# Saving the halves of a key or query tile ahead of the load of the next weight tile, on the SyncE queue of a cross-attention kernel

## The reference

```python
Q = split_heads(query @ Wq.T + bq); K = split_heads(key @ Wk.T + bk); V = split_heads(value @ Wv.T + bv)
scores = einsum('bhqd,bhkd->bhqk', Q, K) / sqrt(32)
scores = where(mask[:, None, :, :] == 0, -1e9, scores)
attn = softmax(scores, axis=-1)
ctx = einsum('bhqk,bhkd->bhqd', attn, V).reshape(B, LQ, H)
x = ctx @ Wo.T + bo + query
out = (x - mean(x)) / sqrt(var(x) + 1e-5) * ln_g + ln_b
```

## Time and profile before

| | |
|---|---|
| median of 3 runs | 1682.52 us (1680.51 to 1682.59) |
| the profiled execution | 1682.58 us, of it the span of the core 1680.8 us |
| TensorE busy (matmul) | 1608.1 us, 96% |
| GpSimd, ScalarE, VectorE busy | 1408.6 us (84%), 1349.6 us (80%), 1168.9 us (70%) |
| granted TensorE clock, mean | 0.983 |
| DMA queue of SyncE, share of 16 engines | 66.5%, 325.94 MB |
| chain that ended last | TensorE 78%, DMA 12% (of it `stack_scratch<-qk_lo` 11%), VectorE 6% |

### The profile page before, as it was taken

One profiled execution on the slowest core, in us unless ns is written; L12 is line 12 of the kernel. 1 busy time (PEld: TensorE's weight loads), 2 busy tenths in 40 slices (PEclk: granted clock), 3 DMA queues, 4 the chain that ended last, 5 costly groups with the idle time before them and its releaser, 6 DMA issues.

```text
span 1680.8 us, 25568 instructions
## 1 busy us (share of the span) xinstructions
PE 1608.1 (96%) x7997; PEld 1029.3 (61%) x7997; DVE 1168.9 (70%) x2852; ACT 1349.6 (80%) x1555; POOL 1408.6 (84%) x875
## 2 busy tenths in 40 slices
PE   7879999999999999999999999999999999999986
PEld 5546666666666666666666666666666666665633
DVE  6647767767777676777767677676777767676744
ACT  3668888887889788788888878888888888878772
POOL 5558888898889989889898988989898997988683
PEclk9999999999999999999999999999999999999977
DMA  7886676776767677586777757667676867757401
GB/s 250 249 252 193 166 225 183 208 220 175 242 164 235 182 214 221 159 241 175 220 197 202 217 166 233 192 209 218 170 231 169 241 179 202 225 171 220 102 9 69
DMA packets 197479, 327.58 MB, mean 195 GB/s; under 512 B 39264, under 2 KB 39264, under 8 KB 197344
## 3 DMA queue, kind: packets, MB, share of 16 engines
q1 hardware_dynamic: 197344, 325.94, 66.5%
HBM read 236.72 MB, written 89.13 MB: 194 GB/s over the span
## 4 chain that ended last, share of the span: by engine, by line
PE 78%; DMA 12%; DVE 6%; POOL 2%; issue 1%; ACT 1%; SPq 0%; DVEq 0%; ACTq 0%; POOLq 0%
PE proj_bank L1099 37%; PE ring L973 12%; PE exp_banks L988 12%; PE ctx_bank L1004 12%; DMA stack_scratch<-qk_lo 11%; DVE qk_lo L817 2%; PE ring L1024 2%; DVE ring L776 2%; PE ring L1033 1%; DVE qk_hi L814 1%; DMA b_all<-ln_b_dram 1%; ACT qk_hi L663 1%; POOL total L497 1%; PE ctx_bank L1099 0%; POOL c_lo L475 0%
## 5 line engine op out<-in xcount | busy, mean ns | idle before, releaser
L776 DVE CUSTOM_DVE_ANT_0 ring<-ring,bias 128x512 f32<-128x512 f32 x1024 | 690.5, 711 | 308.0 <-PE ring L973 306.7
L643 ACT ACTIVATE probs<-exp_banks 128x1024 f32<-128x1024 f32 x512 | 524.5, 1025 | 226.2 <-PE exp_banks L988 223.9
L614 ACT CAST exp_banks<-biasT 128x1024 f32<-128x1024 bf16 x512 | 520.7, 1017 | 23.1
L973 PE MATMUL ring<-k_stack,q_stack 96*128 96x512 f32 x1024 | 333.3, 403 | 15.4 <-DVE maxes L776 10.9
L988 PE MATMUL exp_banks<-q_stack,k_stack 98*128 98x512 f32 x1024 | 327.6, 402 | 3.0 <-ACT exp_banks L614 3.0
L505 POOL TENSOR_TENSOR total<-total,probs 128x1024 f32<-128x1024 f32 x126 | 299.4, 2400 | 10.0 <-ACT probs L643 1.2
L497 POOL TENSOR_TENSOR total<-total,probs 128x2048 f32<-128x2048 f32 x63 | 290.4, 4609 | 11.5 <-ACT probs L643 2.9
L497 POOL TENSOR_TENSOR total<-probs 128x2048 f32<-128x2048 f32 x63 | 289.5, 4596 | 0.0
L1004 PE MATMUL ctx_bank<-probs,v 128*32 128x512 f32 x2048 | 278.5, 616 | 0.7 <-DVE recipT L843 0.7
L973 PEld LDWEIGHTS ring<-k_stack,q_stack 96*128 96x128 f32 x1024 | 194.8, 191 | 75.5 <-DVE maxes L776 25.0
L988 PEld LDWEIGHTS exp_banks<-q_stack,k_stack 98*128 98x128 f32 x1024 | 194.0, 191 | 58.5 <-issue 9.2
(11 more groups left out here) (131 smaller groups left out, 2248.8 us busy)
## 6 DMA issues: line engine op xcount, KB each, us to landing
w_tile<-w_scratch SPq DMA_DIRECT2D x240, 256.0 KB, 3.2
k_stack<-stack_scratch SPq DMA_DIRECT2D x192, 256.0 KB, 4.6
q_stack<-stack_scratch SPq DMA_DIRECT2D x192, 256.0 KB, 6.6
stack_scratch<-qk_hi SPq DMA_DIRECT2D x128, 256.0 KB, 2.9
stack_scratch<-qk_lo SPq DMA_DIRECT2D x128, 256.0 KB, 3.7
c_raw<-cT_dram SPq DMA_DIRECT2D x64, 256.0 KB, 3.7
x_raw<-xT_dram SPq DMA_DIRECT2D x64, 256.0 KB, 4.7
mask_raw<-mask_dram SPq DMA_DIRECT2D x64, 256.0 KB, 4.6
```

What stands on the lines that cost most here:

```text
L614: nc.scalar.copy(exp_banks[:, 2 - 2 * wave:4 - 2 * wave, :], biasT[:, kc:kc + 1, :].to_broadcast([P, 2, L])).then_inc(seeded, 1)
L643: nc.scalar.activation(probs[:, u % PS, 2 - 2 * wave:4 - 2 * wave, :], exp_banks[:, 2 - 2 * wave:4 - 2 * wave, :], ACT.Exp).then_inc(exps, 1)
L776: nc.vector.tensor_tensor_reduce(out=ring[:, n % 2], in0=ring[:, n % 2], in1=bias[:, c], scale=1.0, scalar=LOWEST, op0=ALU.subtract, op1=A ...
L973: nc.tensor.matmul(ring[:, n % 2], q_stack[0:3 * D, at, c * P:(c + 1) * P], k_stack[0:3 * D, at, :], start=True, stop=True).then_inc(ring_ ...
```

## The change

In each step, the halves of tile `y - 1` are now saved ahead of the load of the weights of tile `y + 1`. `load_weights` takes the part as an argument and is called twice in a row; its waits are thereby written twice, the second time already met.

```diff
-            def load_weights(tile):
+            def load_weights(tile, part):
                 i = PLAN.qk[tile]
                 if i < MADE:
                     return
                 sp.wait_ge(proj_done, PLAN.no[PLAN.qk_list[i - WS]] + 1)
                 sp.wait_ge(wk_scratch if tile[0] == "K" else wq_scratch, 2 * FULL)
                 w = (0 if tile[0] == "K" else NG) + tile[2]
-                for part in range(2):
-                    sp.dma_start(w_tile[:, i % WS, part].bitcast(FP32), w_scratch[w, :, part]).then_inc(
-                        w_loaded[i % WS][part], FULL)
+                sp.dma_start(w_tile[:, i % WS, part].bitcast(FP32), w_scratch[w, :, part]).then_inc(
+                    w_loaded[i % WS][part], FULL)
...
                 if PLAN.max_group(y) is not None:
                     store_maxes(PLAN.max_group(y))
-                tile = PLAN.tile(y + 1)
-                if tile and tile[0] in "QK":
-                    load_weights(tile)
                 tile = PLAN.tile(y - 1)
                 if tile and tile[0] in "QK":
                     keep_halves(tile)
                     if PLAN.qk[tile] < 2:
                         stack(tile[0], 0)
+                tile = PLAN.tile(y + 1)
+                if tile and tile[0] in "QK":
+                    load_weights(tile, 0)
+                    load_weights(tile, 1)
```

## The result

The changed kernel takes 1693.1 us, the median of 5 runs (1689.14 to 1698.57), against 1682.52 us before (5 runs, 1679.06 to 1685.25). The ratio is 1.0053, 95% interval 1.0034 to 1.0072: slower by 0.5% (the quotient of the two medians, 1.0063, lies inside the interval). The forecast was 1681.1 us, range 1670 to 1689. The profiled execution took 1693.56 us, its span 1691.8 us.

What follows compares the result with a forecast made beforehand. The prediction took TensorE's work and its waits for `qk_lo` (22.0 us in 27 events) to bound the kernel. Its sum was 1682.58 - 12.7 - 0.8 + 12.0 = 1681.1 us, range 1670 to 1689.

Steps and rivals of the forecast that it cites:

- Positions 6, 8, 9 and 10, other work behind the halves: Maxima, mask and stack loads and row stores go out up to 1 us later; TensorE doesn't wait for them: nothing.
- no change: Forecast verdict, chance 0.47: a difference from the kernel before of less than 0.2% (3.4 us).
- Place A: Position 9, K1 waits for Q1's halves: `qk_lo` lands 1.3 us sooner, TensorE gains 12.7 of 14.3 us.
- Position 10: Halves of K1 pass the weights of Q2; TensorE's two waits there go, gain 0.8 us.
- The weights of K2: At place A, part 0 now stands third of four DMAs but has 1.2 us to spare: costs nothing.
- Place B: Position 13, K3 waits for Q3's halves: batch starts 0.90 us later, costing 15 x 0.8 = 12.0 us; bounds 0, 13.5.
- rival 2: Halves at A land no sooner, B's late start stays: 1682.6 + 12.0 = 1694.6 us, slower; chance 0.13.
- Rivals 1 and 3: 1: B's late batch is made up, 1669.1 us, chance 0.26. 3: K2's weights become A's wait, 1695 us, 0.07.

Runs made afterwards that it cites:

- position 8 alone: The kernel before, with the swap only at position 8 (weights of K2 behind the halves of Q1): 1667.92 us, ratio 0.9919.
- position 6 alone: The kernel before, with the swap only at position 6 (weights of Q1 behind the halves of K0): 1721.15 us, ratio 1.0231.

## Why the prediction was wrong

**The step that failed** is "Positions 6, 8, 9 and 10, other work behind the halves: nothing", with its reason that TensorE has no wait for the loads that go out later. It asked who waits for those loads and not what stands behind them in the queue. At position 6 the weights of Q1 used to move in 4.3 us in which the queue has little else to do (share 0.48 with them, 0.10 without). Now they move in the 4.9 us after that, right ahead of the six DMAs of the stacks, and the halves of Q1 stand behind those. In the sequence shown, Q1's `qk_lo` took 5.9 us before, 3.7 with position 8 alone and 7.0 with position 6 alone; the medians over the 15 sequences are 5.6, 4.0 and 7.4. In the changed kernel the two nearly cancel: 5.9 in that sequence, 5.4 at the median. With position 6 put back as it was, the time is 1685.21 us, and the forecast's "no change" comes out.

**Place A**, gain of 12.7 us: right in mechanism and size when made alone (13.6 us of idle time); in the changed kernel 3.4 us, and this shortfall of 9.3 us is most of the miss.

**Position 10**, 0.8 us: 0.5 us.

**The weights of K2**, costed at nothing: right. Apart from the run that moved K3's part 1, no profile has more than 1.1 us of waits for `w_tile` before the context products.

**Place B**, 12.0 us: right in mechanism and some low, 14.3 us or 0.95 us a sequence, where the batch starts 0.90 us later and `qk_lo` of Q3 lands 1.0 us later after its issue. The allowance of 0.1 us, that a fuller queue would catch up, had no ground. The bound of 13.5 us was short too.

**The rivals.** The time is that of rival 2 (1694.6), but its reason was another. The halves at A could land sooner, and with position 8 alone did; they did not because new work had come ahead. So the section "Latency and other measured facts" of the Trainium skill's page "DMA: Bandwidth & Descriptors", from which rival 2 had its support, decides nothing here: had its 2 us of loaded HBM latency set the landing, it would have held it in the run with position 8 alone as well, amid engines as full (share 1.05 from 812 to 817 us), and there it moved with the order. Rivals 1 and 3 did not come about.

**The sum as it should have been:** 1682.6 - 3.4 - 0.5 + 14.3 = 1693.0 us, against 1693.56 profiled. The 0.6 us left is a balance of 3.6 us more busy time and shorter waits elsewhere, in the first sequence above all.

**What stays open.** That position 6 is the cause is shown; why it costs as much as it does is shown only in part. The sequence above has less backlog than most. In the 14 sequences from the second on, the same three stretches (3.97 us before the issue of K0's `qk_lo` to 12.23 us after it) move 3362 KB before, 3118 in the changed kernel and 3146 with position 6 alone, at the median. The 244 and 216 KB that are missing are 1.0 and 0.9 us at 244 GB/s. With position 6 alone SyncE issues the mask loads and the stacks no later than before (4.3, 5.2 and 6.7 us after that `qk_lo`), only the weights of K1 about 1 us later, so a late issue of the stacks is ruled out. The `q_stack` DMAs then land 8.1 us after issue in place of 6.9, and Q1's `qk_lo` 7.4 us in place of 5.6. So the backlog covers about half of the 1.8 us, and most of the delay is there once the stacks land; the rest is unexplained. That single DMA engines run behind the mean, which the share over all 16 hides, was not tried. Nor is it settled why a `qk_lo` with an idle queue ahead lands in 2.0 us at one place and 4.2 us at another.

## What to carry to other kernels

A transfer moved behind another in a queue is free only if the queue stays empty long enough afterwards. Look for who waits for the moved transfer, and then also for the next burst in the same queue and for who waits at its end; here the halves stood two steps behind the moved weights, and TensorE's wait three. A burst should start with a transfer that can go out at once, and what frees a buffer should go ahead of what is needed late. One condition for a whole loop is worth taking apart by position: the same swap was worth -15 us at one position, +22 and +38 us at two others. These effects do not add: the three come to +45 us, and all five positions together cost 10.6, since the swap at 8 takes away much of the wait that the one at 6 makes.

## What the runs showed of the hardware that was not expected

A stall of TensorE can cost well over its length. With position 6 alone, the stalls of up to 3.5 us, one in each sequence, were followed in 12 of 15 sequences by a stretch in which the granted clock was at 0.5 (1.2 GHz; at 434 to 438 us throughout), and products that had started 0.23 us apart started 0.43 us apart. The groups' mean went from 407 to 424 ns. TensorE's busy time rose by 15.1 us on top of 22.1 us of longer waits. Where K3's part 1 came late, 2.1 to 3.3 us of stall in each sequence went with 22.6 us more of busy time. Shorter stalls did this seldom: in the changed kernel, with stalls at B of 1.4 us on average, the clock fell behind two of them (at 255 and 457 us). The forecast priced a stall at its length.
